# Two arms of a branch on TensorE change places in a two-layer attention and feed-forward kernel

## The reference, cut to what matters

```python
x = x + L0_xattn(_layernorm(x), ctx, ctx, mask, ...)   # mask from the input
x = x + L0_ffn(_layernorm(x), ternary_weight, bias, act_scale)
x = x + L1_xattn(_layernorm(x), ctx, ctx, ...)         # causal mask, built in
x = x + L1_ffn(_layernorm(x), w_gate, w_up, w_down)    # gated, quantized
```

```python
scores = jnp.einsum('bqhd,bkhd->bhqk', qp, kp) / np.sqrt(D_K)
scores = jnp.where(mask[:, None, :, :] == 0, -10000.0, scores)
attn = jax.nn.softmax(scores, axis=-1)
```

## Time and profile before

| what | us |
|---|---|
| median of 3 runs | 1387.24 |
| lowest and highest of the 3 | 1386.72 and 1391.84 |
| the profiled execution's own time | 1385.02 |
| its span, first to last instruction | 1383.3 |
| TensorE busy in the span | 1283.6 (93%) |
| VectorE, ScalarE, GpSimd busy | 976.5, 838.0, 502.6 |

### The profile page before, as it was taken

The page is one execution under the profiler, slowest core; times in us unless marked ns, Lnnn a source line. Parts: engine busy times, 40 slices in busy tenths (PEclk is TensorE's granted clock), DMA queues, the critical chain, the costliest instruction groups (busy, mean ns, idle before and its releaser), DMA issues. The chain is left out here.

```text
span 1383.3 us, 21084 instructions
## 1 busy us (share of the span) xinstructions
PE 1283.6 (93%) x7272; PEld 635.4 (46%) x7272; DVE 976.5 (71%) x1701; ACT 838.0 (61%) x1449; POOL 502.6 (36%) x670
## 2 busy tenths in 40 slices
PE   9999799999999999999999999999998999950798
PEld 5566323334343343444545554555444444420587
DVE  5776598887878878786666788887744436987532
ACT  5455337776777767777565556556653437959432
POOL 4455200235344454434773433333320003639200
PEclk9999869999999999999999999999999999975899
DMA  8999674232424244342343643333110002326222
GB/s 290 376 339 320 232 173 116 79 91 89 126 72 121 78 124 108 87 125 78 96 131 98 197 117 104 99 93 106 33 32 16 1 0 90 138 87 232 61 92 91
DMA packets 88173, 170.74 MB, mean 123 GB/s; under 512 B 14850, under 2 KB 49414, under 8 KB 86534
## 3 DMA queue, kind: packets, MB, share of 16 engines
q1 hardware_dynamic: 87531, 168.16, 39.4%
q10 hardware_dynamic: 539, 1.26, 0.4%
HBM read 108.26 MB, written 60.31 MB: 122 GB/s over the span
## 5 line engine op out<-in xcount | busy, mean ns | idle before, releaser
L1329 DVE TENSOR_REDUCE b_neg_max<-b_score 128x1 f32<-128x512 f32 (+3 forms) x864 | 540.9, 662 | 177.7 <-PE b_score L877 93.6
L1102 ACT ACTIVATE b_probs<-b_exp 128x512 f32<-128x512 f32 (+1 forms) x864 | 463.2, 581 | 281.7 <-PE b_exp L901 281.0
L874 PE MATMUL b_score<-b_k_stack,b_q_stack 97*128 97x512 bf16 (+3 forms) x1024 | 355.9, 351 | 15.1 <-issue 9.2
L901 PE MATMUL b_exp<-b_q_stack,b_k_stack 100*128 100x512 bf16 (+3 forms) x1024 | 344.5, 341 | 6.4 <-ACT b_probs L1102 5.6
L922 PE MATMUL b_av<-b_probs,b_values 128*17 128x512 f32 (+3 forms) x2048 | 228.5, 518 | 3.7 <-POOL b_probs L1200 3.4
L874 PEld LDWEIGHTS b_score<-b_k_stack,b_q_stack 97*128 97x128 bf16 x1024 | 99.8, 98 | 251.0 <-DVE b_neg_max L1329 128.5
L901 PEld LDWEIGHTS b_exp<-b_q_stack,b_k_stack 100*128 100x128 bf16 x1024 | 100.1, 98 | 82.7 <-ACT b_probs L1102 25.1
L1200 POOL TENSOR_SCALAR_AFFINE_SELECT b_probs<-b_probs 128x512 f32<-128x512 f32 x96 | 61.7, 643 | 176.7 <-ACT b_probs L1102 176.2
L1208 POOL CAST b_max_parts<-b_neg_max 128x16 bf16<-128x16 f32 x64 | 13.0, 202 | 286.2 <-DVE b_neg_max L1329 283.9
L877 PE MATMUL b_score<-diag_qk,minus_big 128*128 128x128 bf16 x512 | 112.6, 220 | 0.0
L1756 POOL TENSOR_TENSOR f_hidden<-f_tmp,f_hidden 128x2048 int32<-128x2048 int32 x8 | 44.3, 5531 | 137.7 <-DVE f_tmp L1708 137.7
(11 more groups left out here) (212 smaller groups left out, 1819.8 us busy)
## 6 DMA issues: line engine op xcount, KB each, us to landing
b_q_stack<-s_q SPq DMA_DIRECT2D x384, 64.0 KB
s_k<-a_part_k SPq DMA_DIRECT2D x48, 256.0 KB, 3.3
b_k_stack<-s_k SPq DMA_DIRECT2D x61, 192.0 KB
s_up<-f_up SPq DMA_DIRECT2D x6, 1536.0 KB, 5.0
s_va<-a_va SPq DMA_DIRECT2D x16, 544.0 KB, 5.4
b_values<-s_va SPq DMA_DIRECT2D x16, 544.0 KB, 4.2
a_mask_q<-mask_in SPq DMA_DIRECT2D x8, 1024.0 KB, 8.7
out_dram<-normed SPq DMA_DIRECT2D x16, 512.0 KB, 3.0
```

Of the source, the lines that this page charges most:

```text
L874: mm = pe.matmul(o, q, KS[half][0:R_MAX, h, 0:w], start=True, stop=causal or not general)
L901: mm = pe.matmul(o, k, QS[half][0:NSTACK, h, q0:T], start=True, stop=not masked)
L1102: nc.scalar.activation(probs[kc][:, h0:h0 + m, q0:T], exp_bank[n % RINGS][:, 0:m * w].rearrange("p (h n) -> p h n", h=m), ACT.Exp).then_in ...
L1329: nc.vector.tensor_reduce(neg_max[u][:, qt, h0:h0 + m], score_bank[n % RINGS][:, 0:m * w].rearrange("p (h n) -> p h n", h=m), AX.X, ALU.ma ...
```

## The change

The condition of the `If` is turned round, and the two arms change places. The same instructions are executed for either value of the register, which is zero or one.

```diff
-            with pe.If(const["flag"] > 0):
+            with pe.If(const["flag"] < 1):
+                program(False, SLOTS[:LAYER + 2])
+            with pe.Else():
                 program(True, SLOTS[:LAYER + 2])
-            with pe.Else():
-                program(False, SLOTS[:LAYER + 2])
             program(False, SLOTS[LAYER + 2:])
```

## The result

The changed kernel takes 1392.71 us (median of 20 runs, 1390.32 to 1397.27), the kernel before 1387.26 in as many (1385.18 to 1392.47). The ratio is 1.0034, with a 95% interval of 1.0025 to 1.0043: slower by 5.45 us, where 5.15 were predicted. The profiled execution took 1391.43 against 1385.02. The sum came out right, but its terms did not: the head lost time instead of gaining it, and the join has one hole instead of two.

What follows compares the result with a forecast made beforehand. TensorE, busy 1283.6 of 1383.3 us, was taken to bound the kernel. Head -3.25, holes +3.3 and +3.6, clock +1.7, won back -0.2 gave +5.15 on 1387.24: 1392.4 us, with 8 in 10 between 1386.5 and 1396.5.

Steps and rivals of the forecast that it cites:

- The head: At the If before the first scores: the branch is no longer taken, so TensorE starts earlier, saving 3.25 us.
- 3.72 falls to about 0.08: The If's branch on TensorE, 3.72 us when taken, would cost about 0.08 us, like an untaken loop branch.
- So I let the whole 3.25 through to 191.02: The head's 3.25 us gain would pass undiminished through the early scores to where TensorE begins dense work.
- The first hole: Between slots 31 and 32: the unconditional jump over the general arm leaves TensorE idle 3.3 us (2.8 to 3.8).
- The second hole: Shortly after the join: the target stands near its block's end, so a second instruction fetch costs 3.6 us (3.0 to 4.5).
- My count: From the fetch at 135.6 to the join: 18,669 instructions, 72 blocks of 256 and 237 over, leaving 19 in the join's block.
- The rival of one hole: At the join one fetch is enough: +1.35 us in all, 1388.6; chance 0.24.
- The clock: Behind the join's holes TensorE's clock falls to half for some 3.5 us, costing 1.7 us (0 to 3.5).
- The sum: Whole kernel: head -3.25, holes +3.3 and +3.6, clock +1.7, won back later -0.2, together +5.15 us.

Runs made afterwards that it cites:

- the kernel with 20 unused matmuls: Changed kernel plus 20 never-executed matmuls (40 instructions) at the end of the general arm, moving the join's target: 1397.04 us, ratio 1.0064.
- the hidden jump: Two kernels: both arms whole copies, 24 fillers ahead of the far jump, batch 1 stacks a slot later: 1388.82 us; loads ahead of the maxima moved too: 1385.10.
- the jump at the end: Changed kernel with slots 32 and later written out in both arms, so the far jump comes at the attention's end: 1389.78 us, ratio 1.0017.
- the three kernels that were halted: Changed kernel with 12 unused matmuls (1392.07 us) or 20 (1397.04); kernel before with a far jump over 1536 never-run fillers at the join (1390.76).

## Why the prediction was right, and where it was wrong

**The head.** "3.72 falls to about 0.08" held (0.09), and so did the first score, 3.26 earlier after the barrier for 3.25 predicted. The step that failed is "So I let the whole 3.25 through to 191.02". It followed the scores and VectorE and the queries of the next group, and left out the DMA that the exponents wait for. The earlier trace rows had the warning: a DMA share of 1.03 in 171 to 182. The term was -3.25 and came out at +2.1 between the two profiled executions; +3.3 by the medians where it stands alone. With the loads moved it can be had: the first L901 came 3.2 earlier.

**The first hole.** Predicted 3.3, measured 2.41. An unconditional jump at this distance, which no row of before shows, took 4.39, longer than the 3.72 taken from the earlier trace rows. That the eight matmuls of L922 need only be handed over, and not finished, before the sequencer goes on to the jump is what the kernel after shows: the jump began at 655.12, the first of the eight at 656.21, and the last ended at 657.27. So the jump was reached 2.15 us before the engine ran dry. I had it wait for the semaphore of these eight and placed it at 654.2, 0.5 us ahead of the old 654.66. The two errors partly cancel.

**The second hole.** Predicted 3.6, absent. The mechanism stands, as the kernel with 20 unused matmuls shows; the size of the block's rest was wrong (19 estimated, about 50 measured). My count took blocks of 256 through 72 of them; that was an estimate from the earlier trace rows, and one instruction more or less in a block moves it by 72. It also began at the fetch at 135.6 and counted what the engine had executed, while fetches follow the sequencer: in all twelve far jumps of these traces the second packet starts 0.7 to 2.2 us after the branch has ended. The sequencer was ahead of the engine by 25 to 27 matmuls and weight loads at the join, by 34 at the hidden jump and by 14 at the jump at the end. That could explain most of the missing 31, as an argument; how far ahead it was at 135.6 no run shows, nor the exact size of a block. The rival of one hole had this right, and of its two reasons the first, the count that rests on trailing fetches; the second block does not come with the first.

The page of before has 58 packets of TensorE's instruction queue with 0.95 MB, 16.4 KB each, for 14,544 matmuls and weight loads, 251 a packet. The second packet is seen 3.4 us behind the first in the kernel after, and in the kernel with 20 unused matmuls the engine stood for it.

**The clock.** Predicted 1.7 on two holes of 3, measured 1.4 on one of 2.4 (6.40 - 5.02).

**The sum.** Predicted -3.25 + 3.3 + 3.6 + 1.7 - 0.2 = 5.15. Measured, without the 0.45 of scatter, +2.1 + 2.5 + 1.4 = 6.0 in the profiled executions and 5.45 in the medians. A gain that wasn't there (5.3 off) and a hole that wasn't there (3.6), with the first hole 0.8 smaller, nearly cancel. That 5.45 came so near to 5.15 is luck. The case that happened, one hole, stood at 1388.6 with a chance of 0.24, and none of the cases had the loss at the head.

Open remain two things. Why maxima issued 2.8 us earlier land 2.0 us later is shown only as far as it is due to the loads around them, not which rule of the queue does it. And the packet behind a far jump starts 0.9 to 2.9 us after the branch does, for no reason that the traces show. This delay sets what a jump costs: in all twelve of them the branch ends 2.3 to 2.7 us after its packet has started.

## What to carry to other kernels

A stall ahead of a stretch whose first inputs come through a full DMA queue may cost nothing, as the branch of 3.72 us at this head, with a DMA share of 1.03 behind it; without it the kernel was 3.3 us slower by the medians. Before counting its removal as gain, follow every input of the next dense instruction, the small late DMA above all. A far taken branch on TensorE took 3.3 to 4.5 us here, and 5.4 once, of which 2.0 to 2.4 stayed as a hole at the join. Behind 24 queued fillers and ahead of a wait for VectorE it cost nothing: that wait stayed at 2.16. Ten fillers alone, at the join, did not help (a hole of 2.26 against 2.41). The sequencer was ahead of the engine by at most some 34 matmuls and weight loads at the jumps in these traces.

## What was not expected of the hardware

- The untaken branch of the If took 0.09 us in all seven kernels that have it, a far taken one 3.27 to 4.51, and 5.38 in one case. How long one took went with when its packet started: 1.0 us after the branch in the jump of 3.72, 2.0 in that of 4.39, 2.9 in that of 5.38.
- Each of the twelve far branches ended behind one packet, with the next starting 0.7 to 2.2 us after its end. In the three kernels that were halted, what lies beyond the target's block was executed 3.2 to 3.4 us after the jump's end: five matmuls did not cover that time, the roughly 25 of the kernel after did.
- The small DMAs of the maxima (4 KB each) were delayed in the full queue by what is issued behind them too: 25.7 us after the barrier fell to 22.6 for the first L901 when only later loads moved, and to 20.8 when only earlier ones did.
- The length of a hole of 2.0 to 2.4 us does not decide alone whether the granted clock falls. It fell to 0.50 behind holes of 2.05, 2.26, 2.27, 2.30 and 2.41, the last at a cost of 1.4 us, and stayed at 1.00 behind 2.00. Behind the wait of 2.15 to 2.17 ahead of the last stretch, the same in all kernels but the one with the jump at the end, it stayed at 1.00 in seven and fell 0.4 to 1.4 us after the wait in six.
